# Attention probabilities transposed by a DMA in SBUF instead of by TensorE through a bank

## The reference

```python
x = x + xattn(layernorm(x), ctx, bias, Wq, Wk, Wv, Wp)      # x: 64 x 128 x 128, ctx: 64 x 120 x 128
x = x + ffn(layernorm(x), gate_w, w_gate, w_up, w_down)

def xattn(queries, keys, bias, Wq, Wk, Wv, Wp):             # 16 heads of 64
    q, k, v = split(queries @ Wq.T), split(keys @ Wk.T), split(keys @ Wv.T)
    scores = einsum('bhqd,bhkd->bhqk', q, k) * 128 ** -0.5 + bias
    out = einsum('bhqk,bhkd->bhqd', softmax(scores), v)
    return merge(out) @ Wp.T

def ffn(x, gate_w, w_gate, w_up, w_down):                   # 8 experts of width 512
    affinity = softmax(x @ gate_w.T)                        # per batch each expert takes its 32 best tokens
    gating, idx = top_k(affinity.T, 32)
    h = silu(x[idx] @ w_gate.T) * (x[idx] @ w_up.T)
    return zeros.at[idx].add(gating * (h @ w_down.T))
```

## Time and profile before

| | before |
|---|---|
| time, median of 3 runs | 1197.02 us (1196.4 to 1198.01) |
| span of the profiled execution, first to last instruction | 1194.1 us, 2.9 us under the median; its own time is not listed apart |
| busy share of the span | PE 95%, PEld 81%, DVE 78%, ACT 85%, POOL 56% |
| instructions | 50330 |

### The profile page before, as it was taken

The page is one execution under the profiler, slowest core; times in us unless marked ns, Lnnn a source line. Parts: engine busy times, 40 slices in busy tenths (PEclk is TensorE's granted clock), DMA queues, the critical chain, the costliest instruction groups (busy, mean ns, idle before and its releaser), DMA issues. The chain is left out here.

```text
span 1194.1 us, 50330 instructions
## 1 busy us (share of the span) xinstructions
PE 1133.8 (95%) x15688; PEld 963.1 (81%) x15688; DVE 936.9 (78%) x3847; ACT 1010.4 (85%) x2919; POOL 663.5 (56%) x1149
## 2 busy tenths in 40 slices
PE   3999999999999999999999999999569999999996
PEld 3899999999999999999999999999436666666664
DVE  3888888888888888888888888888685665666553
ACT  3999999999999999999999999999447666666562
POOL 4555555555555555555555555554207767767673
PEclk9999999999999999999999999999869999999998
DMA  3000000000000000000000000000000111111112
GB/s 99 18 18 21 19 15 18 19 15 18 19 15 18 20 15 15 23 15 15 23 15 15 21 17 15 18 19 4 2 1 19 33 48 44 27 53 43 45 54 62
DMA packets 37002, 29.72 MB, mean 25 GB/s; under 512 B 13920, under 2 KB 30304, under 8 KB 36960
## 3 DMA queue, kind: packets, MB, share of 16 engines
q1 hardware_dynamic: 36096, 27.02, 8.6%
q10 hardware_dynamic: 864, 2.16, 0.5%
HBM read 16.58 MB, written 4.19 MB: 17 GB/s over the span
## 5 line engine op out<-in xcount | busy, mean ns | idle before, releaser
L383 ACT ACTIVATE probs<-neg,negmax 128x120 f32<-128x120 f32 x1024 | 322.9, 397 | 2.2 <-DVE negmax L412 0.6
L229 POOL TENSOR_TENSOR v_lo<-v_f,v_hi 120x256 f16<-120x256 f32 x256 | 167.9, 656 | 270.9 <-ACT v_hi L361 152.4
L412 DVE CUSTOM_DVE_ANT_0 neg<-bk_s,bias_sb 128x120 f32<-128x120 f32 x1024 | 228.4, 279 | 88.7 <-PE bk_s L536 80.0
L1101 POOL TENSOR_TENSOR hid<-hid_f,hid 128x512 f16<-128x512 f32 x128 | 167.6, 1313 | 73.7 <-ACT hid L1055 72.8
L422 DVE TENSOR_TENSOR qk_lo<-bk_a,qk_hi 128x496 f16<-128x496 f32 x256 | 171.5, 670 | 7.2 <-ACT qk_hi L346 7.2
L453 DVE TENSOR_TENSOR pT_lo<-bk_t,pT_hi 120x512 f16<-120x512 f32 x256 | 169.9, 664 | 0.3
L545 PE MATMUL bk_t<-ident,probs 128*120 128x128 f32 x1024 | 166.7, 285 | 1.6 <-ACT probs L383 1.6
L346 ACT CAST qk_hi<-bk_a 128x496 f16<-128x496 f32 x256 | 146.6, 572 | 24.6 <-PE bk_a L520 9.7
L375 ACT CAST pT_hi<-bk_t 120x512 f16<-120x512 f32 x256 | 157.5, 615 | 2.4 <-PE bk_t L545 2.4
L621 PE MATMUL bk_y<-wp_sb,oT 128*128 128x128 f32 x1024 | 156.2, 275 | 0.0
L1155 DVE TENSOR_TENSOR hid_f<-bk_u,silu 128x512 f32<-128x512 f32 x128 | 88.3, 690 | 85.4 <-ACT silu L1048 35.0
(11 more groups left out here) (168 smaller groups left out, 3981.7 us busy)
## 6 DMA issues: line engine op xcount, KB each, us to landing
y_all<-y SPq DMA_DIRECT2D x128, 64.0 KB, 2.0
wst<-ffn_w SPq DMA_DIRECT2D x64, 96.0 KB, 1.9
x_sb<-x SPq DMA_DIRECT2D x64, 64.0 KB, 1.8
out<-x_sb SPq DMA_DIRECT2D x16, 256.0 KB, 2.0
ctx_f<-ctx_t SPq DMA_DIRECT2D x64, 60.0 KB, 1.9
w_f<-wqkv_t ACTq DMA_DIRECT2D x3, 512.0 KB, 5.3
wp_sb<-wp_t ACTq DMA_DIRECT2D x1, 512.0 KB, 6.1
bias_sb<-bias ACTq DMA_DIRECT2D x1, 60.0 KB, 6.1
```

The costliest lines, as they stand in the source:

```text
L229: pool.tensor_tensor(v_lo[par][0:K, GH * g:GH * (g + 1), :], v_f[g % 2][0:K, :, :], v_hi[par][0:K, GH * g:GH * (g + 1), 0:DH], ALU.subtrac ...
L383: e = nc.scalar.activation(probs[g % 2][:, i, :], neg[g % 2][:, i, :], ACT.Exp, bias=negmax[g % 2][:, i:i + 1], scale=-1.0)
L412: r = nc.vector.tensor_tensor_reduce(out=neg[g % 2][:, i, :], in0=bk_s[i % 2][:, (i // 2) * K:(i // 2 + 1) * K], in1=bias_sb[:, :], scale= ...
L1101: nc.gpsimd.tensor_tensor(hid[1][par][:, ic, :], hid_f[ic % 2][:, :], hid[0][par][:, ic, :], ALU.subtract).then_inc(hid_lo_ready, 1)
```

## The change

The probabilities are no longer transposed by TensorE. GpSimd casts `probs` of a group to f16 (`upper_parts`, into the first half of `p_parts`), VectorE subtracts this from `probs` into the second half (`p_lo_ready`), and one transposing DMA on SP's queue (`turn`) moves both halves of four heads, 128 x 1024 f16, into `pT`. `p_parts` and `pT` have a buffer for each of the four groups, and the 8 columns beyond the 120 keys are zeroed once. The bank `bk_t` goes. PV comes four groups behind the scores instead of two (`PV_LAG`), the transpose of its output five, the output projection six; the attention has one slot more at its end. The residual addition and its statistics come in step `(PROJ_LAG + 3) % GROUPS`, which is 1, and the work on batch `t - 3` in GpSimd, ScalarE and TensorE becomes that on batch `t - 4`. The loads have two semaphores instead of one, and their order on SP's queue among the transposing DMAs is written out.

The core of the diff:

```diff
 FRONT = 5
-DRAIN = 3
+DRAIN = 4
+PV_LAG = 4
+TURN_LAG = PV_LAG + 1
+PROJ_LAG = PV_LAG + 2
...
-        pT_hi = two("pT_hi", [128, GH, S], F16)
-        pT_lo = two("pT_lo", [128, GH, S], F16)
+        p_parts = [sb(f"p_parts{i}", [S, 2, GH, 128], F16) for i in range(GROUPS)]
+        pT = [sb(f"pT{i}", [128, 2 * GH, S], F16) for i in range(GROUPS)]
...
-        bk_t, bk_a, bk_b, bk_o, bk_x, bk_y = (bank(n) for n in (
-            "bk_t", "bk_a", "bk_b", "bk_o", "bk_x", "bk_y"))
+        bk_a, bk_b, bk_o, bk_x, bk_y = (bank(n) for n in ("bk_a", "bk_b", "bk_o", "bk_x", "bk_y"))
...
+            def load_x(b, par):
+                if some(b):
+                    sp.wait_ge(loaded_xc, 32 * b)
+                    alone(sp)
+                sp.dma_start(x_sb[:, b, :], x[:, b, :]).then_inc(loaded_xc, 16)
+                if some(b - 1):
+                    sp.wait_ge(ctx_ready, b - 1)
+                    alone(sp)
+                sp.dma_start(ctx_f[par][:, :], ctx_t[:, b, :]).then_inc(loaded_xc, 16)
+            def load_ffn(b, par):
+                if some(b):
+                    sp.wait_ge(loaded_ffn, 16 * b)
+                if some(b - 1):
+                    sp.wait_ge(ffnw_ready, b - 1)
+                alone(sp)
+                src = ffn_w[:, bass.ds(b * WCH, WCH)] if not isinstance(b, int) else ffn_w[:, b * WCH:(b + 1) * WCH]
+                sp.dma_start(wst[par][:, :], src).then_inc(loaded_ffn, 16)
+            def turn(t, g):
+                n = 4 * (t - 1) + g
+                sp.wait_ge(p_lo_ready, n + 1)
+                alone(sp)
+                if some(n - GROUPS + 1):
+                    sp.wait_ge(pv_written, n - GROUPS + 1)
+                alone(sp)
+                sp.dma_start_transpose(pT[g][:, :, :], p_parts[g][:, :, :, :].rearrange("p a b c -> p (a b c)")
+                                       ).then_inc(pT_moved[g], 16)
             def slot(t, par):
-                if some(t * 48):
-                    sp.wait_ge(loaded, t * 48)
-                sp.dma_start(x_sb[:, t, :], x[:, t, :]).then_inc(loaded, 16)
-                if some(t - 1):
-                    sp.wait_ge(ctx_ready, t - 1)
-                sp.dma_start(ctx_f[par][:, :], ctx_t[:, t, :]).then_inc(loaded, 16)
-                if some(t - 1):
-                    sp.wait_ge(ffnw_ready, t - 1)
-                src = ffn_w[:, bass.ds(t * WCH, WCH)] if not isinstance(t, int) else ffn_w[:, t * WCH:(t + 1) * WCH]
-                sp.dma_start(wst[par][:, :], src).then_inc(loaded, 16)
-            slots(sp, slot, end=B, first=0)
+                if live(t - 1):
+                    turn(t, 0)
+                if live(t + 2):
+                    load_x(t + 2, par)
+                if live(t - 1):
+                    turn(t, 1)
+                if live(t + 1):
+                    load_ffn(t + 1, (par + 1) % 2)
+                if live(t - 1):
+                    turn(t, 2)
+                    turn(t, 3)
+            load_x(0, 0)
+            slots(sp, slot, end=B + 1, loop_end=loop_end - 2)
...
+            def upper_parts(t, g):
+                if live(t - 1):
+                    n = 4 * (t - 1) + g
+                    pool.wait_ge(probs_ready, n + 1)
+                    if some(t - 1):
+                        pool.wait_ge(pT_moved[g], 16 * (t - 1))
+                    alone(pool)
+                    pool.tensor_copy(p_parts[g][:, 0, :, 0:K], probs[g % 2][:, :, :]).then_inc(p_hi_ready, 1)
...
+                upper_parts(t - 1, GROUPS - 1)
                 values(t - 1, GROUPS - 1, i)
...
+                upper_parts(t, 0)
                 values(t, 0, par)
...
+                upper_parts(t, 1)
                 values(t, 1, par)
...
+                upper_parts(t, 2)
                 values(t, 2, par)
...
-                b1, g1 = behind(t, g, 1)
-                if live(b1):
-
-                    act.wait_ge(pT_written, 4 * b1 + g1 + 1)
-                    if some(4 * b1 + g1 - 1):
-                        act.wait_ge(pv_written, 4 * b1 + g1 - 1)
-                    nc.scalar.copy(pT_hi[g1 % 2][0:K, :, :].rearrange("p a b -> p (a b)"),
-                                   bk_t[0:K, :]).then_inc(pT_hi_ready, 1)
                 if live(t - 1):
                     act.wait_ge(neg_ready, n + 1)
                     if some(n - 1):
-                        act.wait_ge(pT_written, n - 1)
+                        act.wait_ge(p_lo_ready, n - 1)
...
-                    dve.wait_ge(pT_hi_ready, 4 * b1 + g1 + 1)
-                    if some(4 * b1 + g1 - 1):
-                        dve.wait_ge(pv_written, 4 * b1 + g1 - 1)
-                    nc.vector.tensor_tensor(pT_lo[g1 % 2][0:K, :, :].rearrange("p a b -> p (a b)"), bk_t[0:K, :],
-                                            pT_hi[g1 % 2][0:K, :, :].rearrange("p a b -> p (a b)"),
-                                            ALU.subtract).then_inc(pT_lo_ready, 1)
+                    dve.wait_ge(p_hi_ready, 4 * b1 + g1 + 1)
+                    nc.vector.tensor_tensor(p_parts[g1][:, 1, :, 0:K], probs[g1 % 2][:, :, :],
+                                            p_parts[g1][:, 0, :, 0:K], ALU.subtract).then_inc(p_lo_ready, 1)
...
-                if g == GROUPS - 1 and live(t - 2):
-
-                    dve.wait_ge(proj_written, 4 * (t - 2) + 4)
-                    nc.vector.tensor_tensor(x_sb[:, t - 2, :], x_sb[:, t - 2, :], bk_y[:, 0:D],
+                if g == (PROJ_LAG + 3) % GROUPS and live(t - 3):
+
+                    dve.wait_ge(proj_written, 4 * (t - 3) + 4)
+                    nc.vector.tensor_tensor(x_sb[:, t - 3, :], x_sb[:, t - 3, :], bk_y[:, 0:D],
                                             ALU.add).then_inc(x1_ready, 1)
-                    dve.wait_ge(x1_ready, t - 1)
+                    dve.wait_ge(x1_ready, t - 2)
                     alone(dve)
-                    nc.vector.bn_stats(stats[:, 1, :], x_sb[:, t - 2, :]).then_inc(dve_chain, 1)
+                    nc.vector.bn_stats(stats[:, 1, :], x_sb[:, t - 3, :]).then_inc(dve_chain, 1)
...
-                b1, g1 = behind(t, g, 1)
-                if live(b1):
-                    pe.wait_ge(probs_ready, 4 * b1 + g1 + 1)
-                    if some(4 * b1 + g1):
-                        pe.wait_ge(pT_lo_ready, 4 * b1 + g1)
-                    for i in range(GH):
-                        m = nc.tensor.transpose(bk_t[0:K, i * S:(i + 1) * S], probs[g1 % 2][:, i, :], ident[:, :])
-                    m.then_inc(pT_written, 1)
-                b2, g2 = behind(t, g, 2)
+                b2, g2 = behind(t, g, PV_LAG)
                 if live(b2):
-                    p2 = (par + 1) % 2 if g >= 2 else par
-                    pe.wait_ge(pT_lo_ready, 4 * b2 + g2 + 1)
+                    p2 = par
+                    pe.wait_ge(pT_moved[g2], 16 * (b2 + 1))
                     pe.wait_ge(v_lo_ready, 4 * b2 + g2 + 1)
                     if some(4 * b2 + g2):
                         pe.wait_ge(o_ready, 4 * b2 + g2)
                     for i in range(GH):
                         h = GH * g2 + i
-                        ph, pl = pT_hi[g2 % 2][0:K, i, :], pT_lo[g2 % 2][0:K, i, :]
+                        ph, pl = pT[g2][0:K, i, :], pT[g2][0:K, GH + i, :]
```

More of the change, by code:

```diff
@@ L147, in attention @@
         scores_written, neg_ready, probs_ready = sem("scores_written"), sem("neg_ready"), sem("probs_ready")
-        pT_written, pT_hi_ready, pT_lo_ready = sem("pT_written"), sem("pT_hi_ready"), sem("pT_lo_ready")
+        p_hi_ready, p_lo_ready = sem("p_hi_ready"), sem("p_lo_ready")
+        pT_moved = [sem(f"pT_moved{i}") for i in range(GROUPS)]
         pv_written, o_ready = sem("pv_written"), sem("o_ready")
@@ L214, in _ @@
                 pool.memset(v_hi[i][:, :, DH:OW], 1.0).then_inc(const_ready, 1)
+            for i in range(GROUPS):
+                pool.memset(p_parts[i][:, :, :, K:], 0.0).then_inc(const_ready, 1)
             pool.wait_ge(pool_chain, 1)
@@ L300, in before @@
                     return each * (t - lag) if not isinstance(t, int) else each * min(max(t - lag, 0), B)
-                c = 1 + (t + 1) + before(-1, 2) + before(0, 2) + before(3, 1)
+                c = 1 + (t + 1) + before(-1, 2) + before(0, 2) + before(4, 1)
                 out = [c + 1]
-                for batch in (t + 1, t, t + 1, t, t - 3):
+                for batch in (t + 1, t, t + 1, t, t - 4):
                     out.append(out[-1] + (1 if live(batch) else 0))
@@ L324, in step @@
                 tw, gw, pw = (t, g - 1, par) if g else (t - 1, GROUPS - 1, (par + 1) % 2)
-                b4, g4 = behind(t, g, 4)
+                b4, g4 = behind(t, g, PROJ_LAG)
                 if live(b4):
@@ L346, in step @@
                     nc.scalar.copy(qk_hi[pw][:, gw, :], bk_a[:, 0:QK]).then_inc(qk_hi_ready, 1)
-                if gw == GROUPS - 1 and live(tw - 3):
-                    act.wait_ge(logits_written, tw - 2)
+                if gw == GROUPS - 1 and live(tw - 4):
+                    act.wait_ge(logits_written, tw - 3)
```

(20 more changed lines are left out.)

59 lines of the change are left out of this document (29 added, 30 removed).

## The result

The changed kernel takes 1271.4 us (median of 4 runs, 1270.92 to 1271.96) against 1197.46 us: ratio 1.0617, 95% interval 1.0602 to 1.0632. It is slower, and 2.4 us from the predicted time.

The account below looks back on a forecast made before the run. It took TensorE, VectorE and the loop through both as bounds within 0.1 us. Span 1194.1 + 69 for a 14.00 us batch + 3 at the end = 1266, as run median 1269 us; range 1183 to 1330.

Parts of the forecast that it names:

- The late cast and its neighbour in g1: Second of a batch's four head-group steps: VectorE's residual waits for GpSimd's cast, then v_lo holds the SBUF port; 1.33 us.
- Add and statistics in g1: Second head-group step: residual add and statistics move here from g3, growing the step from 3.07 to 3.65 us.
- g2 and g3 at 2.97: Third and fourth head-group steps: the TensorE-VectorE loop neg, qk_lo, projection, scores sets each at 2.97 us.
- The sum: Steady batch: 3.08 + 3.65 + 1.33 + 2 x 2.97 = 14.00 us, 1.12 above 12.88; +69 us over 62 batches.
- The two ends: Start and finish outside the steady batches; the finish gains cast, transfer and two short steps: +3 us, between +1.3 and +6.
- (b): Rival: the transposing DMA sets the pace from 3.5 us a transfer; 5 us gives 1641, 23 us 6100; chance 0.20.
- the middle one of its three cases: Transposing DMA on SP's queue: a transfer cut into 256-byte pieces, 1024 packets, takes 2.9 us.
- (a): Rival: GpSimd's cast comes in time, stall hidden; 12.67 us a batch, 1187 us; chance 0.17 with its like.
- (c): Rival: the cast is late but no SBUF port conflict; 13.05 us a batch, 1211 us; chance 0.13.
- the expected gain: Removing TensorE's transposes (0.49 us a step) and ScalarE's bank copy; by the loop a batch falls at most to 11.88 us.

Follow-up runs that it names:

- the second cut: Kernel before the change, without TensorE's four probability transposes per group and without ScalarE's copy out of bk_t: 1194.97 us (0.9977).
- the third cut: Kernel before the change, without transposes and ScalarE's copy, plus a second v-product bank (bk_b) in place of bk_t: 1164.22 us (0.9731).

## Why the prediction came out right, and where it did not

- **The late cast and its neighbour in g1: shown.** The cast took 0.585 us, estimated at 0.58. Moved forward, it took 53 us off; v_lo alone moved away took 26. The stall was mis-sized: 1.33 predicted, 4.47 - 3.63 = 0.84 measured, half of it waiting and half sharing. Three parts of the 0.49 are seen: vpe was held up by 0.24 us and not 0.42; g0 took 3.15 to 3.23 and not 3.08, so VectorE came later; and the step of 3.63 still has 0.12 of sharing in it. The Trainium skill (SBUF — State Buffer, "Who interferes with whom") also counts tensor_scalar among the operations that can take the port pair shared with GpSimd; the xn of 0.64 beside v_lo and 0.34 without it agrees.
- **Add and statistics in g1: right.** Without the stall g1 is 3.63 us, or 3.51 without that sharing, predicted 3.65; taking bn_stats out of it gave 24 us.
- **g2 and g3 at 2.97: the step that failed.** g2 has it (2.97), g3 takes 3.45. The prediction said that the loop neg, qk_lo, projection, scores sets g2 and g3 once the transposes are gone. For g3 it does not: in the changed kernel with the early cast the batch stays at 13.21 with a second bk_a. What binds g3 is TensorE and ScalarE round the one bank bk_b where the logits share it, 3.44 us in the changed kernel and 3.37 in the second cut; only with that bank doubled do further steps come near 2.97 (3.04 and 2.97 in the third cut). In the ramp, where the 2.97 was read, ScalarE does not yet copy oT, x2T and logits, so the loop through bk_b is shorter there. In the steady batch TensorE, 698 of 700 us busy, showed no wait for v_hi, because the transposes filled the time. ScalarE at 685 was passed over.
- **The sum.** That 14.00 predicted and 14.09 measured agree is partly luck: g1 with its stall was put 0.51 too long (4.98 for 4.47) and g3 0.48 too short, which cancel; g0 was 0.07 to 0.15 too short. The direction was no luck, since the early cast alone gives back 53 us. The two ends cost 3.2 and 3.3 us, predicted together with the extra batches as 5 x 1.12 + 3 = 8.6.
- **The rivals.** (b) is out by the run without DMAs. The transfers land in 3.1 us, just above the 2 to 3 us taken, and neither the 10.5 nor the 1.0 us that the prediction cites came; in some 1056 packets a transfer was cut as in the middle one of its three cases (1024 pieces, 2.9 us). (a) did not come by itself; it needs the cast moved, and even then gives 1218 us and not 1187, because g3 and g0 stay longer. For (c), the late cast without a neighbour, the run with v_lo behind xn gives a batch of 13.66 us, not 13.05; most of the difference is the 0.48 of g3.
- **Where the expected gain went.** Transposes and copy taken out alone are worth 2.9 us, because the loop through bk_b ends where they do. With them out, the bank that comes free is worth 30 us more when it is used for bk_b (21 in the changed kernel with the early cast), and the change left it unused.

## What to carry to other kernels

An engine that is busy all the time need not be the only bound, since its work may fill a wait: take the work out in thought, and look for the loop that remains, for each single buffer through which two in-order engines hand work back and forth. When an instruction gets a new input from another engine, look up what stands ahead of the producer in that engine's order, and which of the two meets whom in SBUF. When two waits cancel in a sum, a good total says little: compare step by step.

## What was new in the hardware's behaviour

- A transpose of 128 x 1024 f16 from SBUF to SBUF by DMA lands 3.1 us after its issue (256 KB, some 1056 packets), against 2.0 us for a store of the same size, and 67 MB more in the queue cost no time: with and without them the kernel takes 1271.4 and 1270.9 us, though the loads of x and of the expert weights land in 2.0 and 2.2 us with them and in 1.8 and 1.9 without.
- A GpSimd subtraction of two SBUF tensors slows not only VectorE's operations with two SBUF inputs (0.63 to 1.10 us) but also its tensor_scalar with one SBUF tensor (0.33 to 0.64); 0.47 us was lost on the residual and, where v_lo met the two xn instead, 0.43 on these. Where VectorE's residual came first, by 0.05 us, it took its 0.63 and GpSimd's cast 0.73 for 0.30.
